# Masked attention scores that accumulate on a mask written by ScalarE, column halves of key and query projections, and a re-derived instruction order

## What is computed

```python
def _attn(q, k, v, mask):
    scale = 1.0 / np.sqrt(HD)
    s = jnp.einsum('bqhd,bkhd->bhqk', q, k) * scale
    s = jnp.where(mask, s, jnp.finfo(s.dtype).min)
    a = jax.nn.softmax(s, axis=-1)
    return jnp.einsum('bhqk,bkhd->bqhd', a, v)
```

## Time and profile before

| | us |
|---|---|
| median of 3 runs (2467.3 to 2474.87) | 2468.3 |
| profiled execution | 2470.3 |
| its span, first to last instruction | 2468.8 |
| PE busy | 2295.3 (93%) |
| DVE busy | 1673.9 (68%) |
| ACT busy | 1265.5 (51%) |
| POOL busy | 372.2 (15%) |
| mean granted clock of PE | 0.962 |

### The profile page before, as it was taken

The page is one execution under the profiler, slowest core; times in us unless marked ns, Lnnn a source line. Parts: engine busy times, 40 slices in busy tenths (PEclk is TensorE's granted clock), DMA queues, the critical chain, the costliest instruction groups (busy, mean ns, idle before and its releaser), DMA issues.

```text
span 2468.8 us, 37030 instructions
## 1 busy us (share of the span) xinstructions
PE 2295.3 (93%) x13127; PEld 1203.3 (49%) x13127; DVE 1673.9 (68%) x5149; ACT 1265.5 (51%) x2434; POOL 372.2 (15%) x409
## 2 busy tenths in 40 slices
PE   6888799989997989999989999998999999999987
PEld 2675355655664645554445555543444343334554
DVE  5677977864335765567877676758786778884563
ACT  2444545542322225555636665645766747776653
POOL 3013533342201100000200010000001010002021
PEclk9999999998997979999989999999999989999998
DMA  6566520000001320101222100042230133110120
GB/s 225 150 188 200 174 70 30 24 12 5 14 2 46 103 33 14 27 31 36 99 67 86 47 29 14 20 139 78 88 57 14 39 109 96 49 36 12 52 73 17
DMA packets 150940, 160.63 MB, mean 65 GB/s; under 512 B 33407, under 2 KB 120274, under 8 KB 150492
## 3 DMA queue, kind: packets, MB, share of 16 engines
q1 hardware_dynamic: 150756, 158.28, 22.1%
HBM read 97.39 MB, written 60.19 MB: 64 GB/s over the span
## 4 chain that ended last, share of the span: by engine, by line
PE 75%; DVE 14%; ACT 3%; DMA 3%; POOL 2%; issue 2%; SPq 1%; DVEq 0%; POOLq 0%; ACTq 0%
PE bank L1251 10%; PE bank L1223 9%; PE bank L1198 9%; PE bank L1785 9%; PE bank L1808 7%; PE bank L1227 4%; PE bank L2291 4%; PE bank L849 3%; PE bank L2471 3%; PE bank L1705 2%; DVE max L1330 2%; PE bank L765 2%; PE bank L2293 2%; PE bank L1061 2%; DVE stats L717 1%
## 5 line engine op out<-in xcount | busy, mean ns | idle before, releaser
L1265 ACT ACTIVATE work<-bank 128x512 f32<-128x512 f32 (+1 forms) x1216 | 687.7, 595 | 381.4 <-PE bank L1227 178.7
L1327 DVE CUSTOM_DVE_ANT_0 bank<-bank,weights 128x512 f32<-128x512 f32 x512 | 348.0, 700 | 122.2 <-PE bank L1198 120.5
L1198 PE MATMUL bank<-k_stack,q_stack 97*128 97x512 bf16 x896 | 354.8, 401 | 34.5 <-DVE max L1330 16.5
L1330 DVE TENSOR_REDUCE max<-bank 128x1 f32<-128x512 f32 x512 | 335.1, 684 | 62.4 <-PE bank L1198 58.9
L1223 PE MATMUL bank<-q_stack,k_stack 99*128 99x512 bf16 x896 | 339.2, 383 | 2.5 <-ACT work L1265 2.0
L1785 PE MATMUL bank<-hT,weights 128*128 128x512 f32 x512 | 255.7, 613 | 5.5 <-ACT work L1835 2.9
L1198 PEld LDWEIGHTS bank<-k_stack,q_stack 97*128 97x128 bf16 x896 | 88.1, 98 | 246.3 <-DVE max L1330 109.1
L1227 PEld LDWEIGHTS bank<-ident_b,weights 128*128 128x128 bf16 x2048 | 157.8, 97 | 102.5 <-issue 8.8
L1808 PE MATMUL bank<-weights,work 128*128 128x256 f32 x768 | 195.3, 384 | 3.8 <-DVE work L1875 3.5
L1227 PE MATMUL bank<-ident_b,weights 128*128 128x128 bf16 x2048 | 198.0, 218 | 0.0
L1808 PEld LDWEIGHTS bank<-weights,work 128*128 128x128 f32 x768 | 140.9, 190 | 68.1 <-issue 29.8
(11 more groups left out here) (232 smaller groups left out, 3617.8 us busy)
## 6 DMA issues: line engine op xcount, KB each, us to landing
q_stack<-parts_q SPq DMA_DIRECT2D x60, 384.0 KB, 4.0
parts_q<-parts SPq DMA_DIRECT2D x46, 384.0 KB, 2.5
k_stack<-parts_k SPq DMA_DIRECT2D x40, 384.0 KB, 4.8
weights<-parts_q SPq DMA_DIRECT2D x36, 384.0 KB, 3.5
parts_q<-parts SPq DMA_DIRECT2D x46, 256.0 KB, 2.9
parts_k<-parts SPq DMA_DIRECT2D x24, 384.0 KB, 2.6
parts_k<-parts SPq DMA_DIRECT2D x24, 256.0 KB, 2.9
weights<-in_L_e_w SPq DMA_DIRECT2D x12, 512.0 KB, 5.8
```

Source lines behind the costliest of these rows:

```text
L1198: m = pe.e.matmul(bank.ap[:, :], self.q(g)[0:MAX_ROW, h, qt * P:(qt + 1) * P], k_stacks[self.key, g].ap[0:MAX_ROW, h, half * BLK:(half + 1 ...
L1265: ac.e.activation(p.ap[0:self.nk, :], banks[self.key, "exp", g, i].ap[0:self.nk, :], ACT.Exp).then_inc(*probs.tick((self.key, g, i)))
L1327: ve.e.tensor_tensor_reduce(bank[:, :], bank[:, :], mask_bias[:, qt, half * BLK:(half + 1) * BLK], 1.0, -3.4e38, ALU.add, ALU.max, to).the ...
L1330: ve.e.tensor_reduce(to, bank[:, :], AX_X, ALU.max).then_inc(*maxima.tick((self.key, g, i)))
```

## The change

Three things are edited, and the order of every engine is derived anew.

**The mask.** A new stage `MaskTurn` follows `Mask` in lane A. PE transposes the part of the bias that belongs to queries of token half 0 (32 matmuls), and ACT copies it, scaled back to 0 or 1, as bytes into SBUF (8 instructions). `MaskCopy` copies these bytes once more by DMA for batch 1, since the first place is used again by the query stacks of the cross attention. In self2, for each exp tile of half 0, ACT writes the transposed mask, scaled by -2^100, into the tile's bank right after the exp of the tile two before it. The score matmul then accumulates onto the bank (`start=False`), and the four L1227 matmuls are left out. Tiles of half 1 stay as they were. `QueryRows` moves to the next phase and also waits for the copy and for the end of self2 of batch 0; the first cross attention load of L2 waits for it.

**Column halves.** `PartsOf` runs one channel half of a `Parts` stage. In L0 (both batches) and for batch 0 of L2, the order becomes k half 0, q half 0, k half 1, loads of the first groups (in L0 batch 1 they stay behind V), q half 1.

**Buffers.** The queries of L0 get two parts buffers of their own (4 and 5), which lie where the weights of L0's MLP are loaded later; that load waits for their last stores.

```diff
 ORDER = {
     "tensor": (
...
-            wC[:, at:at + 768].bitcast(BF16).rearrange("p (r s) -> p r s", r=PARTS) for at in (6144, 6912)])
+            wC[:, at:at + 768].bitcast(BF16).rearrange("p (r s) -> p r s", r=PARTS) for at in (6144, 6912, 0, 768)])
...
+        masked_of = [wC[:, at:at + 1024].bitcast(U8).rearrange("p (t q) -> p t q", t=NT) for at in (5120, 10240)]
...
+        class PartsOf(Stage):
+            def __init__(self, parts, c):
+                self.parts, self.cs, self.beats = parts, (c,), parts.beats
+
+            def tensor(self, pe):
+                return self.parts.tensor(pe, self.cs)
...
-                for f in bank.free:
-                    pe.wait_ge(*f)
+                written = self.mask and half == 0
+                if written:
+                    pe.wait_ge(*evac[self.key, "masked", g, i])
+                else:
+                    for f in bank.free:
+                        pe.wait_ge(*f)
...
-                    m = pe.e.matmul(bank.ap[0:self.nk, :], self.k(g, h, STACK, kt * P), q, start=True, stop=not self.mask)
-                    if self.mask:
+                    m = pe.e.matmul(bank.ap[0:self.nk, :], self.k(g, h, STACK, kt * P), q, start=not written,
+                                    stop=written or not self.mask, skip_group_check=written)
+                    if self.mask and not written:
                         pe.wait_ge(*vec["mask"])
...
+                        if self.mask and (g, i) == (0, 0):
+                            for first in range(2):
+                                self.write_mask(ac, 0, first)
+                                yield
...
+                        n = g * self.n + i + 2
+                        if self.mask and n < self.groups * self.n and self.head_half(n % self.n)[1] == 0:
+                            self.write_mask(ac, n // self.n, n % self.n)
+                            yield
...
+            def write_mask(self, ac, g, i):
+                bank = banks[self.key, "exp", g, i]
+                for f in bank.free:
+                    ac.wait_ge(*f)
+                for done, key in self.mask:
+                    ac.wait_ge(*done[key])
+                ac.e.activation(bank.ap[:, :], masked_of[self.b][:, i // 4, :], ACT.Copy, scale=MASKED).then_inc(
+                    *evac.tick((self.key, "masked", g, i)))
...
+        class MaskTurn(Stage):
+            beats = NT + 1
+
+            def tensor(self, pe):
+                for kt in range(NT):
...
+                    pe.wait_ge(*vec["mask"])
+                    for t in range(TPB):
+                        m = pe.e.matmul(bank.ap[:, t * P:(t + 1) * P], mask_bias[:, t, kt * P:(kt + 1) * P], ident_b[:, :],
+                                        start=True, stop=True)
...
+            def scalar(self, ac):
+                yield
+                for kt in range(NT):
+                    ac.wait_ge(*dense["mask_turn", kt])
+                    ac.e.activation(masked_of[0][:, kt, :], banks["mask_turn", kt].ap[:, :], ACT.Copy, scale=1.0 / MASKED).then_inc(
...
+        class MaskCopy(Stage):
...
+            def sync(self, sp):
+                for done, key in self.after:
+                    sp.wait_ge(*done[key])
+                sp.wait_ge(*evac["mask_turned"])
+                sp.e.dma_start(masked_of[1], masked_of[0]).then_inc(*ld_mask.tick("copy"))
...
-            st["q"] = Parts(lane_d, b, "L0", "q", st["n1"], "L0qkv", 0, 0.25, quarter(0), ("bq", 0), (), pace=b + 1)
+            st["q"] = Parts(lane_d, b, "L0", "q", st["n1"], "L0qkv", 0, 0.25, quarter(0), ("bq", 0), (), pace=b + 1, slots_at=(4, 5))
...
+        def halves(b, keys, queries, *begin):
+            k, q = S_[b][keys], S_[b][queries]
+            return [PartsOf(k, 0), PartsOf(q, 0), PartsOf(k, 1), *begin, PartsOf(q, 1)]
...
-            ([mods["L0"]], [StackRows(), early(0, "v")] + of(0, "n1") + [ValueOnes()] + of(0, "k", "q") + [begin_win] + of(0, "v"), [Rest(3), LoadTokens(1), Rest(1)]),
-            (of(0, "win"), [early(0, "so"), early(1, "v")] + of(1, "n1", "k") + [context0] + of(1, "q", "v") + [begin_win1],
+            ([mods["L0"]], [StackRows(), early(0, "v")] + of(0, "n1") + [ValueOnes()] + halves(0, "k", "q", begin_win) + of(0, "v"), [Rest(3), LoadTokens(1), Rest(1)]),
+            (of(0, "win"), [early(0, "so"), early(1, "v")] + of(1, "n1") + halves(1, "k", "q")[:2] + [context0] + halves(1, "k", "q")[2:] + of(1, "v") + [begin_win1],
...
-            ([mask, load_l2co] + of(0, "n4", "k2", "q2") + [begin_self] + of(0, "v2") + [context2], of(1, ("e", 0, "n"), ("e", 0))),
-            (of(0, "self2"), of(1, ("e", 1, "n"), ("e", 1)) + [v_high2] + of(1, "n4", "k2", "q2", "v2") + [query_rows, early(0, "so2"), begin_self1],
+            ([mask, load_l2co, mask_turn] + of(0, "n4") + halves(0, "k2", "q2", begin_self) + of(0, "v2") + [context2], of(1, ("e", 0, "n"), ("e", 0))),
+            (of(0, "self2"), of(1, ("e", 1, "n"), ("e", 1)) + [v_high2, mask_copy] + of(1, "n4", "k2", "q2", "v2") + [early(0, "so2"), begin_self1],
...
```

More of the change, by code:

```diff
@@ L360, in build_program @@
         ld_tm = [count(f"ld_tm{b}", 16) for b in range(B)]
-        st_parts = [count(f"st_parts{i}", 16) for i in range(4)]
+        st_parts = [count(f"st_parts{i}", 16) for i in range(6)]
         ld_kx = [count(f"ld_kx{b}", 16) for b in range(B)]
@@ L829, in __init__, with turns, tensor @@
                 self.beats = 2 * pace * (len(self.items) + 1)
+            def turns(self, cs):
+                return [(n, c, bl) for n, (c, bl) in enumerate(self.items) if c in cs]
             def stored(self, c):
                 return [st_parts[self.slots_at[n % 2]][self.key, c, bl] for n, (ci, bl) in enumerate(self.items) if ci == c]
-            def tensor(self, pe):
+            def tensor(self, pe, cs=range(CC)):
                 w = wt[self.wname]
-                for n, (c, bl) in enumerate(self.items):
+                for n, c, bl in self.turns(cs):
                     k = (self.key, c, bl)
@@ L875, in scalar, with pool @@
                     yield from rest(2 * self.pace)
-            def pool(self, po):
+            def pool(self, po, cs=range(CC)):
                 yield from rest(2 * self.pace)
-                for c, bl in self.items:
+                for _, c, bl in self.turns(cs):
                     if self.rope:
@@ L887, in pool, with vector @@
                     yield from rest(2 * self.pace)
-            def vector(self, ve):
+            def vector(self, ve, cs=range(CC)):
                 yield from rest(2 * self.pace)
-                for c, bl in self.items:
+                for _, c, bl in self.turns(cs):
                     yield from self.split(ve, c, bl)
@@ L2774, in build_program @@
             st["self2"] = Attention(lane_a, b, "L2", "full", st["q2"], st["k2"], (V, V_high)[b], [(vec, (st["v2"].key, "all"))],
-                                    [(dense, (st["v2"].key, "all"))], rows_ready=k_rows, keys_ready=[], mask=True, period=40, stacks=(0, 1),
+                                    [(dense, (st["v2"].key, "all"))], rows_ready=k_rows, keys_ready=[],
+                                    mask=[((evac, "mask_turned"), (ld_mask, "copy"))[b]], period=40, stacks=(0, 1),
                                     stacks_free={i: [(pool_done, k_rows[i])] for i in range(2)},
@@ L2873, in build_program @@
         third = KeyRows("third", [third_k], [third_q], [(exp_scores, (two_["self2"].key, 7, 31)), (maxima, (two_["self2"].key, 7, 31))])
-        query_rows = QueryRows([(vec, ((two_["q2"].key, 1, 1), "sum"))])
+        query_rows = QueryRows([(vec, ((two_["q2"].key, 1, 1), "sum")), (ld_mask, "copy"),
+                                (exp_scores, (one_["self2"].key, GROUPS - 1, one_["self2"].n - 1))])
+        mask_turn, mask_copy = MaskTurn(), MaskCopy(after_l1)
         v_high2 = Ones("V_high_ones2", V_high, after_l1)
@@ L2924, in sync_program @@
             sp.wait_ge(*st_mod["L3"])
-            for i in range(4):
+            for i in range(6):
                 sp.wait_ge(*st_parts[i]["all"])
```

98 lines of the change are left out of this document (59 added, 39 removed).

## The result

| | before | after |
|---|---|---|
| median (5 runs each, same chip), us | 2473.27 | 2454.07 |
| ratio, 95% interval | | 0.9913, 0.9895 to 0.9931 |
| profiled span, us | 2468.8 | 2452.8 |

The change makes the kernel faster by 0.9%, some 21 us, where 58 were forecast. The direction is right, the size is not, and the time lies above the upper end of the range (2450). Part of that is the base: it was 2468.3 when the forecast was made. The ratio on that base gives 2447, at the slow end of the range, near rival (a); the 2395 to 2435 that the forecast gave 0.65 are missed either way.

A forecast was written before the change was run, and what follows sets the result against it. PE's issue rate was taken to bound the masked attentions. The terms -56 + 8 + 2 - 7 - 5 = -58 on 2470.3 us, less 2 for the median, gave 2410 us; range 2384 to 2450, with 0.65 on 2395 to 2435.

The forecast's parts named there:

- rival (a): Masked attentions: ACT paces them mildly, 0.12 us of PE per write, parts 4 and 5 give nothing; 2445 us, chance 0.13.
- part 1: Masked attentions: 1024 mask matmuls of half 0 leave PE and give back their pitch, -56 us.
- part 2: Masked attentions: 256 mask writes on ACT, mostly covered by PE's other work, +8 us, 0.03 us each.
- 1 us of slack: Masked attentions: a bank's turn of four tiles costs 2.8 us and fits within the 3.78 us that four tiles take.
- start to start price on ACT: Masked attentions: each mask write taken at 0.52 us of ACT, bounds 0.48 and 0.63.
- Part 3: Making the transposed mask: 32 more matmuls and 8 ACT copies, +2 us, bounds 0 and 5.
- Part 4: L0: halves and own query slots take two store waits, 7.1 us, off the chain; -7 us, bounds 0 and 14.
- Part 5: First ramp, before self2 of batch 0: halves and new order move the softmax chain under PE-bound work, -5 us.
- a small permutation, priced 0 +- 8: Whole kernel: everything else in the new order was taken to cost or gain 0 +- 8 us.
- (b): Masked attentions: write queueing idles PE, so the clock grant drops to a mean of 0.85; slower, 2520 us, chance 0.07.
- (c): Whole kernel: the re-derived order gives back elsewhere, for instance in the second ramp, what attentions gain; 2465 us, chance 0.05.
- (d): Attentions and ramps: the ACT cost is covered and both ramps give their upper ends; 2380 us, chance 0.10.

The follow-up runs named there:

- e1: The changed kernel with its new order, halves and buffers, but no mask writes and all mask matmuls kept; ratio to the kernel before 1.0008.
- e2: The changed kernel without the mask writes and without the 1024 mask matmuls on tiles of half 0; ratio to the kernel before 0.9823.
- e11: The kernel before, in its old order, without the mask matmuls on tiles of half 0 and with no writes; ratio to the kernel before 0.9917.
- e3: e2 with 256 ACT operations of the write's size, going to an SBUF scratch tile and waiting for nothing new; ratio to the kernel before 0.9885.
- e4: e3 with each added ACT operation also waiting for the exp just before it, while PE doesn't wait for it; ratio to the kernel before 0.9927.

## Why the prediction was wrong, point by point

By ratios times 2475 us, the sum reads:

| step | forecast | measured | from |
|---|---|---|---|
| parts 3, 4, 5 | -10 | +2 (+-4) | e1 |
| part 1 | -56 | -46 (+-6) | e1 to e2 |
| part 2 | +8 | +22 (+-6) | e2 to after |
| sum | -58 | -22 (+-5) | after |

**What bounds the kernel.** "A matmul taken out gives back its pitch, as long as no other engine moves into its place" was true, but I took the busy share for the proof that none was near. The busy time of a matmul row (0.38 us) is longer than its pitch (0.22), so stalls up to 0.16 us don't show on PE. They show on PEld, its weight loads, which I didn't read. What PEld waited for, from 866 to 1643 us in both kernels, which is self2 of both batches with its ramps before and roughly that in after (us in total, times, longest), before:

```profile
PEld bank L1198 <- DVE max L1327: 80.1, 96, 4.6
PEld bank L1223 <- ACT work L1265: 39.2, 148, 0.9
```

and after:

```profile
PEld bank L1224 <- DVE max L1375: 103.9, 148, 4.9
PEld bank L1253 <- ACT bank L1318: 55.7, 101, 1.0
PEld bank L1253 <- ACT work L1300: 51.9, 114, 1.0
```

These waits lie partly beside matmuls and are no sum of time lost, and of the 80.1 us before 55.7 lie outside the ramps, but they name the two neighbours, DVE's maximum and the exp, that the turns then showed at 3.65 and 3.60 us.

**Part 1.** The pitch was right: 0.49 us for a turn's eight matmuls, where 0.44 to 0.46 came from the earlier trace rows. What failed is that it is given back everywhere. In plain turns of the new order it gave 0.12 at most; in e2 the 1024 matmuls are worth 46 us for 56, in the old order (e11) 21.

**Part 2.** The durations held: 602 ns, and 0.54 us from a write to the next exp. The step that failed is the chain with "1 us of slack". I counted a bank's turn (exps, a write, scores) as 2.8 us against a turn of 3.78, as if nothing else of PE were in it. But PE is in order, and between the scores of two exp tiles stand max tiles and PV; with them the loop is 4.26 us, 0.5 *above* the turn. There is no slack, and the writes cost 0.66 us in a plain turn (3.60 to 4.26), where 0.03 each, 0.06 a turn, was forecast. The view that had it was the one I had used: write the loop down from the timeline of PE, with every instruction between, not the members of the dependence alone. The second miss is the start to start price on ACT: 0.52 us was taken from two exps that don't wait for each other, while a write waits for the exp just ahead, which makes 0.63. Rival (a) came closest in size, 2445, and is right that the writes queue; its 0.12 us a write is 31 us against 22. It priced parts 4 and 5 at nothing, which is what e1 gives. But its reason, an ACT that is nearly full, isn't the cause.

**Part 3.** No run isolates it; it is inside e1's +2 (+-4) with parts 4 and 5.

**Part 4** was right: both stores left the chain, and the window starts 9.0 us earlier, 7 forecast. Over all kernels with it self2 starts some 11 us earlier, so it isn't lost on the way; it is given back in self2 when the matmuls stay on PE (e1).

**Part 5** was wrong. The first ramp is 50.5 us against 48.7, its clock 0.70 against 0.68. And "a small permutation, priced 0 +- 8" was the largest term of all, in both signs: with the writes, order, halves and buffers together decide between 0.9% faster and 1.7% slower, and with all matmuls on PE (e1) the new order eats what part 4 gains (self2 10.4 us longer). No run has the new order without the halves, so the two aren't told apart. Rivals (b), (c) and (d) didn't come: the clock held at 1.00 in both attentions.

## What to carry to other kernels

Before an operation is moved to an idle engine, write the loop down that it joins, with everything that an in-order engine issues between its members, and set the loop's length beside the distance at which the work repeats; average load says nothing of it. Where matmuls overlap, read the waits of the weight loads: a PE that is 99% busy can have two other loops within 5% of it. And when a change comes with a new order, ask which turns are plain and which are filled, since a floor costs in the first and can be free in the second.

## What the hardware showed that I had not expected

- An ACT instruction that waits for the end of the one just ahead of it starts 629 ns after it (128x512, median, in after), one that doesn't 494 ns (e3). The Trainium skill ("ScalarE: Activation LUTs", What ACT_TABLE_LOAD costs) says that back-to-back ACTIVATEs overlap by about 93 ns; the trace agrees: in e3 an exp of 599 ns (mean) and the operation behind it start 494 ns apart, some 100 ns of overlap. Here the wait costs 135 ns.
- Bytes from SBUF to float32 in a bank take 601 ns (median), bytes to bytes in SBUF 621 in e3 and 629 in e4, all 128x512. Place and type of the result differ together, so these 20 to 28 ns can't be put down to one of them.
- Repeating turns lock in. Of 96 turns of the changed kernel 53 are 4.26 us to within 0.02, with a block of other work of PE in them or none.
